# Replicating the first layer's result on TensorE for the first two chunks of a DLRM tower kernel, with a reordered start

## The reference

```python
def _cin_layer(h, h0, W, b):
    Wr = W.reshape(W.shape[0], Hn, Mn)
    x = jnp.einsum('bhd,bmd,ohm->bod', h, h0, Wr) + b[None, :, None]
    return jax.nn.relu(x)
e = jnp.stack([tbl_0[ids[:, 0]], ..., tbl_31[ids[:, 31]]], axis=1)   # 1024 x 32 x 64
x1 = _cin_layer(e, e, W1, b1)                    # 128 outputs
direct2 = _cin_layer(x1[:, :64], e, W2, b2)      # 128 outputs
z = jnp.sum(concat([x1[:, 64:], direct2], axis=1), axis=-1)
h = relu(concat([z, dense_ctx], axis=1) @ W_top1 + b_top1)
y = relu(h @ W_top2 + b_top2) @ W_top3
```

## Time and profile before

| | us |
|---|---|
| median of the runs | 2021.38 |
| the profiled execution | 2020.18 |
| its span | 2018.4 |
| PE busy | 1991.0 (99%) |
| DVE busy | 1920.1 (95%) |
| ACT busy | 1671.3 (83%) |
| POOL busy | 1370.3 (68%) |

### The profile page before, as it was taken

The page is one execution under the profiler, slowest core; times in us unless marked ns, Lnnn a source line. Parts: engine busy times, 40 slices in busy tenths (PEclk is TensorE's granted clock), DMA queues, the critical chain, the costliest instruction groups (busy, mean ns, idle before and its releaser), DMA issues.

```text
span 2018.4 us, 24272 instructions
## 1 busy us (share of the span) xinstructions
PE 1991.0 (99%) x7030; PEld 1322.2 (66%) x7030; DVE 1920.1 (95%) x672; ACT 1671.3 (83%) x4953; POOL 1370.3 (68%) x647
## 2 busy tenths in 40 slices
PE   5999999999999999999999999999999999999999
PEld 3666666666666666666666666666666666666664
DVE  6999999999999999999999999999999999999992
ACT  3888888888888888888888888888888888888884
POOL 5767867777677767768667668677767768677520
PEclk9999999999999999999999999999999999999999
DMA  7999999989989999999999999999999999998960
GB/s 214 261 262 245 263 239 243 259 240 243 258 240 243 254 244 243 252 247 242 250 250 241 249 252 240 248 251 241 249 251 239 247 253 240 247 254 240 244 174 11
DMA packets 272119, 482.57 MB, mean 239 GB/s; under 512 B 37473, under 2 KB 70753, under 8 KB 271858
## 3 DMA queue, kind: packets, MB, share of 16 engines
q1 hardware_dynamic: 244786, 404.58, 66.7%
q0 software_dynamic: 26624, 75.52, 21.7%
q10 hardware_dynamic: 576, 0.92, 0.1%
HBM read 313.10 MB, written 16.78 MB: 163 GB/s over the span
## 4 chain that ended last, share of the span: by engine, by line
PE 97%; DMA 1%; POOL 1%; issue 0%; SPq 0%; ACT 0%; DVE 0%; POOLq 0%; ACTq 0%
PE acc L618 21%; PE acc L630 19%; PE acc L637 19%; PE acc L631 19%; PE acc L642 16%; PE acc L621 1%; POOL gathered L272 0%; DMA plo_dma<-pnear 0%; PE x1p L721 0%; PE acc L721 0%; DMA gathered<-in_tables,idx_all 0%; DMA x1rep<-x 0%; DMA near<-emb_rows 0%; PE acc L728 0%; PE x1p L600 0%
## 5 line engine op out<-in xcount | busy, mean ns | idle before, releaser
L305 POOL TENSOR_TENSOR prod<-near,h 128x2048 f32<-128x2048 f32 x126 | 581.5, 4615 | 442.3 <-DMA near<-emb_rows 287.7
L630 PE MATMUL acc<-phi,w2lo 128*128 128x512 f32 x1664 | 704.4, 423 | 0.9 <-ACT phi L838 0.9
L631 PE MATMUL acc<-phi,w2hi 128*128 128x512 f32 x1664 | 651.8, 392 | 0.0
L534 DVE TENSOR_TENSOR pnear<-near,x1p 128x2048 f32<-128x2048 f32 x254 | 568.8, 2282 | 3.2 <-DMA plo_dma<-pnear 3.1
L527 DVE TENSOR_TENSOR pfar<-far,x1p 128x4096 f32<-128x4096 f32 x128 | 565.3, 4417 | 0.0
L272 POOL DMA_INDIRECT gathered<-in_tables,idx_all x256 | 495.5, 1935 | 71.5 <-issue 68.2
L845 ACT CAST phi<-pfar 128x2560 fp32r<-128x2560 f32 x128 | 300.2, 2345 | 216.5 <-PE acc L631 183.6
L618 PE MATMUL acc<-prod,w1T 128*128 128x512 f32 x1024 | 460.2, 592 | 1.5 <-DVE prod L507 1.5
L538 DVE TENSOR_TENSOR plo<-pnear,phi 128x3072 fp32r<-128x3072 f32 x128 | 433.5, 3386 | 0.0
L538 DVE TENSOR_TENSOR plo<-pfar,phi 128x2560 fp32r<-128x2560 f32 x128 | 361.7, 2826 | 41.1 <-ACT phi L845 40.7
L630 PEld LDWEIGHTS acc<-phi,w2lo 128*128 128x128 f32 x1664 | 313.1, 188 | 96.5 <-issue 30.4
(11 more groups left out here) (77 smaller groups left out, 1258.6 us busy)
## 6 DMA issues: line engine op xcount, KB each, us to landing
far<-emb_rows SPq DMA_DIRECT2D x512, 256.0 KB, 4.1
near<-emb_rows SPq DMA_DIRECT2D x510, 256.0 KB
plo_dma<-pnear POOLq DMA_DIRECT2D x128, 512.0 KB
x1rep<-x SPq DMA_DIRECT2D x255, 256.0 KB
h<-emb_rows SPq DMA_DIRECT2D x128, 256.0 KB
emb_rows<-gathered SPq DMA_DIRECT2D x127, 128.0 KB
rem_parts<-rem_hi SPq DMA_DIRECT2D x128, 64.0 KB
gathered<-in_tables,idx_all POOLq DMA_INDIRECT x256
```

What stands on the lines that cost most here:

```text
L305: nc.gpsimd.tensor_tensor(prod1[:, :, :], near[(u + 2) % 3][:, :, :], h0[odd][:, :].unsqueeze(1).to_broadcast([P, K1, N]), ALU.mult).then_ ...
L534: return nc.vector.tensor_tensor(pnear[:, a, :, :], near[u % 3][:, :, :], factor.unsqueeze(1).to_broadcast([P, K1, N]), ALU.mult)
L630: nc.tensor.matmul(acc2[s][:, :], w2lo[:, t, :], phi[:, t, :], start=(t == T_DMA), stop=False)
L631: mm = nc.tensor.matmul(acc2[s][:, :], w2hi[:, t, :], phi[:, t, :], start=False, stop=(t == T_SPLIT - 1))
```

## The change

1. **x1rep by TensorE for chunks 0 and 1.** A matrix `sel` of ones and zeros (in the space of `wt1b`, made by two DVE copies) is multiplied with x1's 64 rows, one fp32 matmul for each half, straight into `x1p`. The DMAs and ACT's copy go for these two chunks. From chunk 2 on the DMAs remain.
2. **near(0) in two halves.** `h0` and the tiles 0 and 1 of chunk 0 have a semaphore of their own, `near_first`, for the first half of DVE's products.
3. **Layer 1 moved.** Layer 1 of chunk 1 moves from ahead of step 0 into step 0; that of chunk 2 from step 0 to step 1, where that of chunk 3 stays, behind the near part of `low`. GpSimd's product of chunk 2 waits for DVE's last low part of step 0. ACT's `early_x1` and `late_sums` now serve chunks 0 to 3.
4. **The start reordered.** The turns of `dense` and DVE's copies of them (to `z1`) go first; pair 0's remainder products are made between the gathers of pair 1, pair 2's gathers go to step 0; `place_remainder(0)` and `load_far(0, 0)` go ahead of pair 1's store on SP.

Its core (`...` is left out):

```diff
+        sel = wt1b[0:H, 0:A2 * P].rearrange("r (a p) -> r a p", a=A2)
...
POOL, step:
+                if at <= 1:
+                    low_parts(c)
+                if at == 0:
+                    for g in range(PAIR_GATHERS):
+                        gather(g, 2, 2)
+
+                    pool.wait_ge(lo_far_ready, 1)
                 if within(at, 2):
 
                     pool.wait_ge(acc1_ready, c + 2)
...
SP, ahead of the steps:
-            load_h0(sp, 0, 0, 0)
-            load_near_tiles(sp, 0, 0, range(0, K1 // 2))
+            load_h0(sp, 0, 0, near_first)
+            load_near_tile(sp, 0, 0, 1, near_first)
             load_near(sp, N, 1, 1)
+            place_remainder(0)
+            load_far(0, 0)
             store_rows(1, 1, 1)
             move_upper(1, 1)
-            place_remainder(0)
-            load_far(0, 0)
             sp.wait_ge(emb_stored, 2 * STORES)
-            sp.wait_ge(x1_early, 1)
-            replicate_x1(sp, [0])
-
-            sp.wait_ge(x1rep_in, 16 * A2)
...
+            def next_x1rep(c):
+
+                if c <= 2:
+                    sp.wait_ge(x1_early, c + 2)
+                else:
+                    sp.wait_ge(z1_ready, c + 2)
+                if c >= 2:
+                    sp.wait_ge(x1p_ready, c - 1)
+                replicate_x1(sp, range(A2))
...
DVE, ahead of the steps:
+            dve.wait_ge(near_first, FIRST)
+            products1(0, slice(0, K1 // 2)).then_inc(p1_first, 1)
+            dve.wait_ge(near_in[0], loads(0, 1))
+            products1(0, slice(K1 // 2, K1)).then_inc(p1_ready, 1)
+            for n in range(1, len(PARTS)):
                 low_weights(n)
...
DVE, step:
                 for a in range(A2):
+                    if at <= 1:
+                        dve.wait_ge(x1p_half, A2 * c + a + 1)
                     near_half(c, u, a).then_inc(pnear_ready, 1)
                 if at == 0:
-                    dve.wait_ge(x1p_ready, 1)
+
+                    dve.wait_ge(acc1_ready, 1)
+                    dve.wait_ge(near_in[1], LOADS)
+                    products1(1, slice(0, K1)).then_inc(p1_ready, 1)
...
PE:
+            def replicate(c):
+
+                for h in range(A2):
+                    nc.tensor.matmul(x1p[c][:, h * N:(h + 1) * N], sel[:, h, :], x1[0:H, :], start=True, stop=True).then_inc(x1p_half, 1)
+
...
+                if at == 1:
+                    pe.wait_ge(p1_ready, 4)
+                    pe.wait_ge(z1_ready, 2)
+                    layer1(1, 1)
...
ACT, step:
-                if within(at, 1):
+                if at >= 3 and within(at, 1):
                     act.wait_ge(acc1_ready, c + 2)
 
-                    act.wait_ge(x1rep_in, 16 * A2 * c + 16 * A2)
-                    if at == 0:
-                        early_x1(1)
-                    else:
-                        layer1(c + 1, 1 - odd)
+                    act.wait_ge(x1rep_in, 16 * A2 * (c - 1))
+                    layer1(c + 1, 1 - odd)
...
+                if at <= 2:
+                    act.wait_ge(acc1_ready, c + 2)
+
+                    if at <= 1:
+                        act.wait_ge(x1p_half, A2 * c + A2)
+                    else:
+                        act.wait_ge(x1rep_in, 16 * A2)
+                    early_x1(1 - odd)
                 act.wait_ge(pfar_ready, c + 1)
...
-                if at == 0:
-                    late_sums(1, 1)
+                if at <= 2:
+                    act.wait_ge(x1_early, c + 2)
+                    late_sums(c + 1, 1 - odd)
```

More of the change, by code:

```diff
@@ L452, in _ @@
                 "p (g r) -> p g r", g=PAIR_GATHERS), table_row[:, :], None, ALU.add).then_inc(idx_all_ready, 1)
+            dve.wait_ge(ident_ready, 1)
+            for a2 in range(A2):
+                ones = ident[0:H, F * a2:F * (a2 + 1)].unsqueeze(2).to_broadcast([H, F, SH])
+                last = nc.vector.tensor_copy(sel[:, a2, :].rearrange("r (i q) -> r i q", q=SH), ones)
+            last.then_inc(sel_ready, 1)
+            dve.wait_ge(top_zero, 1)
+            for h in range(2):
+                dve.wait_ge(tp_filled, 1 + h)
+                nc.vector.tensor_copy(z1[0:DENSE, h * N:(h + 1) * N], tp[h][0:DENSE, :]).then_inc(tp_copied, 1)
             dve.wait_ge(w1_in, 16)
@@ L590, in turn @@
                 mm.then_inc(tp_filled, 1)
+            pe.wait_ge(small_in, 16 * SMALL_DMAS)
+            for h in range(2):
+                turn(h, *DENSE_TURNS[h])
             pe.wait_ge(w1_staged, 1)
-            turn(0, *W1_TURN)
+            turn(2, *W1_TURN)
             pe.wait_ge(w1_second, 1)
-            turn(1, *REM_TURN)
+            turn(3, *REM_TURN)
             def top1(n):
@@ L601, in top1 @@
                 nc.tensor.matmul(acc[:, :], wt1b[:, mc], z2[:, cols], start=False, stop=True).then_inc(top_mm, 1)
-            pe.wait_ge(small_in, 16 * SMALL_DMAS)
-            for h in range(2):
-                turn(2 + h, *DENSE_TURNS[h])
             pe.wait_ge(far_staged, 1)
@@ L693, in step @@
                     top1(3)
-                if begun(at):
+                if at == 0:
+                    pe.wait_ge(hi_dma_ready, 1)
+                    high(odd, range(0, T_DMA)).then_inc(hi_dma_used, 1)
+                    pe.wait_ge(pfar_ready, 1)
+                    whole(odd).then_inc(far_used, 1)
+                    pe.wait_ge(tp_copied, N_TURNS)
+                    pe.wait_ge(x1_early, 2)
+                    replicate(1)
+                else:
                     pe.wait_ge(pfar_ready, c + 1)
@@ L794, in _ @@
             last.then_inc(near_staged, 1)
-            high_weights(0)
-            high_weights(1)
+            for n in range(3):
+                high_weights(n)
             act.wait_ge(small_in, 16 * SMALL_DMAS)
@@ L799, in _ @@
             early_x1(0)
+            high_weights(3)
             act.wait_ge(x1_early, 1)
-            replicate_x1(nc.scalar, [1])
-            for n in range(2, len(PARTS)):
-                high_weights(n)
-            late_sums(0, 0)
+            for b in range(CB // 2):
+                relu_row(acc1[0], acc1[0], bias1, sums1, 0, b)
             remainder_hi(1)
```

137 lines of the change are left out of this document (63 added, 74 removed).

## The result

Seven runs of each kernel on one chip: 2027.48 us after (2026.78 to 2028.43), 2020.34 us before (2019.37 to 2021.54). The ratio is 1.0035, interval 1.0024 to 1.0047: slower by 7 us, above the 0.2% that can be told apart. The profiled execution spans 2025.7 us (before 2018.4).

The account below looks back on a forecast made before the run. PE's matmuls were taken to bound the kernel, so only the start could win. Layer 1 of step 3 0.2 us later plus 0.8 for the clock gave 1.0 later: 2021.2 profiled, 2022.4 us median, range 2016.5 to 2028.

Parts of the forecast that it names:

- rival (b): x1rep transfers of chunks 2 and 3 queue, taking 8.55 us instead of 5.5 each: 6 later, 2028.4 us; chance 0.15.
- The bound and the fixed point: PE's matmuls set the pace; the kernel's end moves as much as layer 1 of step 3, before at 95.62 us.
- Up to step 0: From the start to ACT's first plo_dma: at 30.9 us against 38.56, so 7.7 us earlier.
- end at 26.3: Chunk 0's layer 1: second half of products ready about 24.6, then two matmuls of 0.86 end at 26.3 us.
- Step 0 to 1: From plo_dma of step 0 to that of step 1: the latter at 48.9 us against 58.97, 10.1 earlier.
- step 1 to 2: From plo_dma of step 1 to that of step 2: the latter at 70.9 us against 73.70, only 2.8 earlier.
- Step 2 to 3: ACT needs 18.9 us instead of 14.73; plo_dma of step 3 is 1.4 us later, layer 1 0.2 us later.
- x1rep 5.5: On ACT's line in step 2, chunk 3's x1rep transfer takes 5.5 us.
- The clock: After step 3's waits, matmuls of 0.23 take 0.43 us for some 3 us: 0 to 1.6 lost, taken as 0.8.
- POOL beside DVE: GpSimd's product of chunk 3 meets DVE's far low part in step 1; DVE ends near 66.4, not 64.5, hidden.
- My signs: Expected: pnear at 28 to 30, plo_dma about 31, 49, 71, 90, layer 1 within 2 us of 95.6, ACT-bound waits.
- rival (a): PE carries the early start through without stopping from step 1: 6.7 us earlier, 2014.7; chance 0.15 with what lies towards it.

Follow-up runs that it names:

- e2: The changed kernel plus six discarded products of ident on PE between the fourth and fifth transposing turns; 2024.94 us, 1.0021 of the kernel before.
- e1: The changed kernel with x1 of chunk 3 made at the front of the third step, ahead of plo_dma; 2021.69 us, 1.0007 of the kernel before.
- e3: The changed kernel plus four idle products on PE ahead of the fourth step's high part; 2026.26 us, 1.0032 of the kernel before.
- e4: The kernel before with only TensorE's replication of x1rep for chunks 0 and 1, order otherwise kept; 2014.22 us, 0.9970 of the kernel before.
- e7: e4 with POOL issuing the accumulating DMA of plo_dma ahead of its products in the first step; 2014.09 us, 0.9962 of the kernel before.
- e12: The changed kernel without the wait for DVE's low parts that holds POOL's products of chunk 2; 2028.44 us, 1.0039 of the kernel before.
- e5: The changed kernel with the first layers of chunks 1 to 3, and the order that goes with them, put back; 2019.70 us, 0.9993 of before.
- e9: e5 with the four gathers of pair 2 moved from POOL's first step to behind its first rem_lo; 2014.07 us, 0.9967 of the kernel before.
- e11: The changed kernel with only the four gathers of pair 2 moved behind POOL's first rem_lo; 2027.28 us, 1.0033 of the kernel before.
- e10: e9 plus six products of ident on PE between the fourth and fifth transposing turns; 2013.77 us, 0.9966 of the kernel before.

## Why the prediction was right or wrong

I forecast 2022.4 us and gave 2016.5 to 2028 as the range. 2027.48 lies in it, near its end, 5.1 us over the forecast, and outside the forecast's own 2019 to 2026. That it is slower by more than 0.2% had 0.22; no change, which had 0.63, did not come. That the time lies in the range is partly luck: only the share given to rival (b) had stretched it that far, and the kernel before, measured again, took 2020.34 and not the 2021.38 that the forecast was built on. Against it I forecast 1.0 us more and 7.1 came. The place of the loss was the forecast one, ACT's line around x1rep in steps 1 and 2; the start, one transfer and the clock were sized wrong.

- **The bound and the fixed point** held: no wait of PE from 110 to 2000 us in the changed kernel, and the span moved with layer 1 of step 3, to 0.1 us in all but three profiles. I had that point at 95.8 and 0.8 for the clock; it came at 102.70, 6.1 us later. Of this 3.3 arose up to step 0, 2.2 in step 2 to 3 and 1.0 by the clock, less 0.4 in between.
- **Up to step 0** I had `plo_dma` at 30.9, 7.7 us earlier; it came at 34.23, 4.3 earlier. The staging began 0.3 us later, not 0.7, but ended at 20.61, not 20.1: DVE's copies to pnear and pfar took 1.75 and 1.17 us, before 1.22 and 0.76. So the products began at 22.59 (expected 22.1). From x1 to pnear the working held (1.35 us, expected 1.4). The failed term is layer 1 of chunk 0, "end at 26.3". It began at 23.86, when the first half of the products was there, and at full pace, in e2, its remainder began at 27.05, so some 0.9 us of the 3.3 have nothing to do with the pace: the products were 0.5 us late, and my sum let only two of the four matmuls (3.43 us) stand behind the second half, though the first half comes too late for the other two to be done by then. Most of the rest is that it ran at half pace and took 2.1 us more (5.69 against 3.6). The idle PE at 18 to 20 us, which the removed `keep_running(2)` and the moved dense turns left behind, was in no step of mine. e2 shows it: filling it makes the replication 2.0 us earlier (28.72 against 30.70) and `plo_dma` 1.4.
- **Step 0 to 1** took 17.95 us against 18.0, **step 1 to 2** 21.65 against 22.0: right. The second includes an x1rep transfer of 5.1, expected 5.5.
- **Step 2 to 3** took 21.10 against 18.9. The failed term is "x1rep 5.5": ACT could copy it 7.8 us after its issue (79.23 to 87.04), which was 1.4 us behind the accumulating DMA issued at 77.80. That is rival (b), for one of the two transfers. In e1, issued 1.8 us earlier, it was hidden altogether.
- **The clock**: I took 0.8 of 1.6. It read 0.50 for all of 97 to 103 and was worth the whole: from `plo_dma` to layer 1 passed 7.77 us, against 6.0 in my steps and 6.09 in e3, where the clock kept 1.00. I also had it wrong that the low clock cost nothing before. PE had no wait behind 56.57 there, so its 1.8 us (estimated under e4) were in the time of the kernel before.
- **POOL beside DVE**: the far low part of step 1 took 4.38 us instead of 2.83, hidden as forecast. e7 and e12 show the same effect where nothing hides it.
- **My signs.** ACT was idle ahead of both copies (2.88 and 5.61 us), PE waited for ACT in steps 2 and 3, and nothing waited after 110 us. pnear's first half at 28 to 30 (it came at 31.91) and layer 1 within 2 us of 95.6 did not come. PE's waits in steps 2 and 3 add up to 6.7 us, just under the 7 that I had set as the sign of rival (b).
- **What I had not priced** is the parts apart. The replication by itself was worth 6.3 us (e4), and the new order cost 13.3 on top of it (2014.22 to 2027.48). I asked only what the whole change did. My rival (a), 2014.7, was nearly the time of e4: it needed the order of before.

The reason for the large loss is one rule of the program. Before, layer 1 stood two chunks ahead, so x1, its replication and the products were made while PE worked on the step before. With chunk c + 1's layer 1 inside step c, high part, layer 1, x1, replication, pnear and the next high part form one line, of 17.95 us for step 0, where a step of PE's work is 15.19, and of over 21 where the replication is still a DMA. e5 and e9 show it by taking the layers back, with e11 as the control for the gathers. The best kernels here, e4, e7, e9 and e10 at 2013.8 to 2014.2, beat both the kernel before and the changed one by 0.3% and 0.7%; they can't be told from one another. Of the start's part (near(0) in halves, dense turns first) no gain and no loss is left at the end: e9 has it and e4 doesn't.
